# Linear attention: the denominators are read by VectorE ahead of phi's maximum instead of by ScalarE

## What is computed

```python
def elu_plus_one(x): return jax.nn.elu(x) + 1.0
sq = elu_plus_one(q)                            # q: 16 heads of 128
sk = elu_plus_one(k)                            # k, v: 4 heads, repeated over 16
kv = jnp.einsum('bhsd,bhse->bhde', sk, v)
qkv = jnp.einsum('bhsd,bhde->bhse', sq, kv)
k_sum = sk.sum(axis=2)
norm = jnp.einsum('bhsd,bhd->bhs', sq, k_sum)
attn = qkv / (norm[..., None] + EPS)            # EPS = 1e-6
return attn.transpose(0, 2, 1, 3).reshape(b, s, H * D) @ Wo.T
```

## Time and profile before

| | |
|---|---|
| median of 3 runs | 3480.19 us (3477.25 to 3481.44) |
| the profiled execution's own time | 3482.58 us |
| its span in the trace | 3480.7 us |
| mean granted TensorE clock | 0.986 |
| TensorE busy | 3326.6 us (96%), 19406 matmuls |
| VectorE busy | 2671.6 us (77%) |
| ScalarE busy | 2048.8 us (59%) |
| GpSimd busy | 1057.3 us (30%) |
| chain that ended last | TensorE 71%, VectorE 6%, ScalarE 3% of the span |

### The profile page before, as it was taken

One profiled execution on the slowest core, in us unless ns is written; L12 is line 12 of the kernel. 1 busy time (PEld: TensorE's weight loads), 2 busy tenths in 40 slices (PEclk: granted clock), 3 DMA queues, 4 the chain that ended last, 5 costly groups with the idle time before them and its releaser, 6 DMA issues.

```text
span 3480.7 us, 52744 instructions
## 1 busy us (share of the span) xinstructions
PE 3326.6 (96%) x19406; PEld 2853.0 (82%) x19406; DVE 2671.6 (77%) x4949; ACT 2048.8 (59%) x3904; POOL 1057.3 (30%) x1274
## 2 busy tenths in 40 slices
PE   4899999989999999999999999999999999999995
PEld 3778788768888888888888888888888888888884
DVE  5898896767876787876788677886788767876776
ACT  3677777645556565556555656555555565556552
POOL 4786667622222112122121222212212131212112
PEclk8999999999999999999999999999999999999997
DMA  2221122110000000000000001000000010001000
GB/s 85 73 81 58 54 66 73 50 37 13 13 22 29 15 13 13 15 25 25 13 13 13 28 26 33 13 16 25 25 13 16 14 32 25 16 19 31 27 17 20
DMA packets 98525, 104.21 MB, mean 30 GB/s; under 512 B 10336, under 2 KB 88800, under 8 KB 98144
## 3 DMA queue, kind: packets, MB, share of 16 engines
q1 hardware_dynamic: 98272, 100.85, 9.3%
HBM read 87.18 MB, written 13.63 MB: 29 GB/s over the span
## 4 chain that ended last, share of the span: by engine, by line
PE 71%; DVE 6%; ACT 3%; issue 0%; DMA 0%; POOL 0%; DVEq 0%; SPq 0%; ACTq 0%; POOLq 0%
PE at_ps_job L1965 12%; PE at_ps_job L35 7%; PE at_ps_job L37 7%; PE at_ps_job L36 7%; PE at_ps_o L35 6%; PE at_ps_o L37 6%; PE at_ps_o L36 6%; PE at_ps_s L35 6%; PE at_ps_s L36 6%; PE at_ps_s L37 6%; DVE at_neg_max L1892 1%; ACT x_resident L1716 1%; DVE at_probT_lo L1759 1%; PE at_ps_job L646 1%; DVE at_oT_lo L1790 0%; DVE ch_r L97 0%
## 5 line engine op out<-in xcount | busy, mean ns | idle before, releaser
L1675 ACT ACTIVATE at_probT_hi<-at_ps_job 128x512 fp32r<-128x512 f32 x1024 | 611.8, 598 | 888.9 <-PE at_ps_job L1965 886.5
L1759 DVE TENSOR_TENSOR at_probT_lo<-at_ps_job,at_probT_hi 128x512 fp32r<-128x512 f32 x1024 | 703.0, 687 | 274.8 <-ACT at_probT_hi L1675 264.6
L1716 ACT ACTIVATE x_resident<-at_ps_s,at_neg_max 128x1024 f32<-128x1024 f32 x512 | 570.9, 1115 | 151.4 <-DVE at_neg_max L1892 146.3
L1892 DVE TENSOR_REDUCE at_neg_max<-at_ps_s 128x1 f32<-128x1024 f32 x512 | 622.4, 1216 | 5.2
L1965 PE MATMUL at_ps_job<-ident,x_resident 128*128 128x128 f32 x4096 | 613.7, 272 | 5.0 <-DVE at_probT_lo L1759 3.2
L1965 PEld LDWEIGHTS at_ps_job<-ident,x_resident 128*128 128x128 f32 x4096 | 496.0, 140 | 97.7 <-issue 7.4
L35 PE MATMUL at_ps_o<-at_probT_hi,at_v_lo 128*128 128x512 f32 x1024 | 446.3, 436 | 8.9 <-DVE at_oT_lo L1790 7.8
L1651 POOL TENSOR_TENSOR at_w_hi<-at_w_raw,ch_cols 128x256 fp32r<-128x256 f32 x192 | 117.6, 613 | 1107.0 <-PE at_ps_job L37 1086.2
L35 PE MATMUL at_ps_s<-at_k_hi,at_q_lo 128*128 128x512 f32 x1024 | 445.1, 435 | 0.0
L37 PE MATMUL at_ps_o<-at_probT_lo,at_v_hi 128*128 128x512 f32 x1024 | 404.6, 395 | 0.0
L36 PE MATMUL at_ps_s<-at_k_hi,at_q_hi 128*128 128x512 f32 x1024 | 402.0, 393 | 0.0
(11 more groups left out here) (350 smaller groups left out, 7467.3 us busy)
## 6 DMA issues: line engine op xcount, KB each, us to landing
at_w_raw<-attn_w SPq DMA_DIRECT2D x256, 128.0 KB, 2.3
at_w_raw<-mlp_w SPq DMA_DIRECT2D x112, 128.0 KB, 2.3
li_wo_hi<-li_wo_kept SPq DMA_DIRECT2D x24, 256.0 KB, 2.6
li_wo_lo<-li_wo_kept SPq DMA_DIRECT2D x24, 256.0 KB, 3.0
li_wq_hi<-li_wq_kept SPq DMA_DIRECT2D x48, 128.0 KB, 2.1
li_wq_lo<-li_wq_kept SPq DMA_DIRECT2D x48, 128.0 KB, 2.3
x_resident<-x SPq DMA_DIRECT2D x4, 1024.0 KB, 12.6
out<-x_resident SPq DMA_DIRECT2D x4, 1024.0 KB, 5.0
```

The costliest lines, as they stand in the source:

```text
L1675: nc.scalar.activation(ph[:, i // TC, 4 * half:4 * half + 4, (i % TC) * P:(i % TC + 1) * P], c.turned_bank(2 * TB * u + 2 * i + half), ACT ...
L1716: nc.scalar.activation(prob[:, slot % 2, :], ps_s[slot % 2][:], ACT.Exp, bias=nmax[:, slot:slot + 1], accum_out=rsum[:, u % 2, slot:slot + ...
L1759: nc.vector.tensor_tensor(pl[at], c.turned_bank(2 * TB * u + 2 * i + half), ph[at].bitcast(F32), ALU.subtract).then_inc(s_pl, 1)
L1892: nc.vector.tensor_reduce(nmax[:, slot:slot + 1], ps_s[slot % 2][:], AX.X, ALU.max, negate=True).then_inc(s_max, 1)
```

## The change

The denominators are taken out of PSUM by VectorE (an addition of 1e-6 in place of ScalarE's copy with a bias), their reciprocal is made right behind that, and both now stand ahead of phi's maximum, so that VectorE waits for `s_y` (the end of the outputs' matmuls of the same step) before the maximum. ScalarE's instructions for the denominators go. `rnorm` gets two slots, by the parity of m, so the reciprocal waits for uses of two steps ago in place of those of one step ago. `s_norm` now counts tiles, four for each step.

```diff
-        rnorm = sb("rnorm", [P, TC], F32)
+        rnorm = sb("rnorm", [P, 2, TC], F32)
 # ScalarE
-                if y_step(t):
-                    act.wait_ge(s_y, t - LAG + 1)
-                    if t > LAG:
-                        act.wait_ge(s_rn, t - LAG)
-                    for own, banks in out_banks(t - LAG):
-                        last = nc.scalar.activation(norm[:, own], ps[:, banks, D], ACT.Copy, bias=ATT_EPS)
-                    last.then_inc(s_norm, 1)
...
-                    nc.scalar.activation(ybuf[:, m % 2, :], c.own_bank(("OUT", m, 3))[:, 0:D], ACT.Copy, scale=rnorm[:, 3:4]).then_inc(s_y3, 1)
+                    nc.scalar.activation(ybuf[:, m % 2, :], c.own_bank(("OUT", m, 3))[:, 0:D], ACT.Copy,
+                                         scale=rnorm[:, m % 2, 3:4]).then_inc(s_y3, 1)
 # VectorE
                 dve_background(nc, dve, sh, c, t)
+                if y_step(t):
+                    m = t - LAG
+                    dve.wait_ge(s_y, m + 1)
+                    for own, banks in out_banks(m):
+                        nc.vector.tensor_scalar(norm[:, own], ps[:, banks, D], ATT_EPS, None, ALU.add).then_inc(s_norm, own.stop - own.start)
+                    dve.wait_ge(s_norm, TC * (m + 1))
+                    if m >= 2:
+                        dve.wait_ge(s_y3, m - 1)
+                        dve.wait_ge(s_x, 3 * m - 3)
+                    nc.vector.reciprocal(rnorm[:, m % 2, :], norm[:]).then_inc(s_rn, 1)
                 if q_step(t):
                     dve.wait_ge(s_eq, t + 1)
                     nc.vector.scalar_tensor_tensor(f[:, t % 2, :], ...).then_inc(s_f, 1)
                 if y_step(t):
                     m = t - LAG
-                    dve.wait_ge(s_norm, m + 1)
-                    if m:
-                        dve.wait_ge(s_y3, m)
-                        dve.wait_ge(s_x, 3 * m)
-                    nc.vector.reciprocal(rnorm[:], norm[:]).then_inc(s_rn, 1)
                     dve.wait_ge(s_rn, m + 1)
                     for j in range(3):
                         x = x_tile_of(m, j)
-                        nc.vector.scalar_tensor_tensor(x, ..., rnorm[:, j:j + 1], x, ALU.mult, ALU.add).then_inc(s_x, 1)
+                        nc.vector.scalar_tensor_tensor(x, ..., rnorm[:, m % 2, j:j + 1], x, ALU.mult, ALU.add).then_inc(s_x, 1)
```

More of the change, by code:

```diff
@@ L1307, in _ @@
                         x = x_tile_of(m, j)
-                        nc.vector.scalar_tensor_tensor(x, c.own_bank(("OUT", m, j))[:, 0:D], rnorm[:, j:j + 1], x, ALU.mult, ALU.add).then_inc(s_x, 1)
+                        nc.vector.scalar_tensor_tensor(x, c.own_bank(("OUT", m, j))[:, 0:D], rnorm[:, m % 2, j:j + 1], x, ALU.mult, ALU.add).then_inc(s_x, 1)
         @block.tensor
```

## The result

The changed kernel takes 3470.47 us (median of 7 runs, 3467.94 to 3472.59) against 3480.35 us of the kernel before on the same chip: ratio 0.9971, 95% interval 0.9960 to 0.9981, so 9.9 us less. The forecast was 3481.2 us, the range began at 3471.0, and the time of the rival on the fast side was 3469. The phase behind the loop, and the clock (0.986 in both), are unchanged; the whole gain lies in the loop. Between the first and the last maximum it grows bit by bit: 0.8 us at step 8, 2.3 at step 43, 5.8 at step 71, 9.9 at the last.

A forecast was written before the change was run, and what follows sets the result against it. TensorE was taken to bound the loop at 93% busy, leaking at its wait for phi's maximum. Late steps +4.9, entries +1.1, closed output groups -2.4 and late exponentials -2.0 gave +1.6, taken as +1: 3481.2 us, range 3471 to 3491.

The forecast's parts named there:

- the rival on the fast side: Loop through ScalarE (maximum, copy, Relu, exponential) sets the pace, output groups close up: 12 us less, 3469 us, chance 0.13.
- the other 76: Of the loop's 128 steps, those where VectorE doesn't wait for the exponential and is late behind evictions and background work.
- 45 x 0.14 - 16 x 0.09 = +4.9 us: About 61 steps in late stretches that end in a TensorE wait: 45 without M longer, 16 with M shorter.
- The copy, the next step's Relu and exponential come 0.14 us earlier in a late step: ScalarE: phi's copy starts 0.78 us behind the maximum instead of 1.23, while the maximum starts 0.31 us later.
- nine steps, as -2.0 us: Gated steps with a late exponential: ScalarE's earlier copy gives up to 9 x -0.44 = -4.0 us; half taken.
- The terms of VectorE: Add to reciprocal 0.19 us, reciprocal to maximum 0.12, add to maximum 0.31 or 0.39, maximum to outputs 0.66.
- M: Eviction L1248, once in 32 steps: VectorE's wait for ScalarE's `m_hi` goes; -0.11 us per late step with it.
- The added wait: VectorE waits for the last output matmul (`s_y`) ahead of the maximum; the wait itself costs at most 0.07 us.
- TensorE's wait for `li_f` stays at 30 to 38 us: Sign to check: TensorE's wait for phi's maximum, 34.5 us before; a move over 7 us would refute the forecast.
- 44 us are all that any order of the other engines can give back: Loop with queries, 98 to 700 us: TensorE busy 557.75 of 602 us, so at most 44 us to gain.
- The slower one: VectorE's queue sets the late stretches and the added instructions are serial: 0.28 us per late step, 3491 us, chance 0.17.
- The lower bound: Added instructions free and all of the ScalarE gain arrives: -2.4 - 4.0 = -6.4 us, so 3474 us.

The follow-up runs named there:

- experiment 5: `ybuf` moved on ScalarE to just ahead of the next step's Relu: changed kernel 3472.92 us, kernel before 3465.04; behind the next exponential, kernel before: 3519.46.
- experiment 1's first kernel: Changed kernel with one wait more: ScalarE makes `ybuf`, and then phi's rounding copy, only behind the same step's maximum; 3489.04 us, ratio 1.0025.
- experiment 3: Halves of the change on the kernel before: reciprocal ahead of the maximum, ScalarE's copies kept, 3464.56 us; only the adds on VectorE, behind the maximum, 3494.58 us.

## Why the prediction was wrong, point by point

**"So in the other 76 it reaches the maximum late by itself."** This is the step that failed. I took VectorE's busy time for its work, and a late step's length for the sum of VectorE's own terms: "45 x 0.14 - 16 x 0.09 = +4.9 us". But VectorE's late arrival hangs in part on the maximum of the step before, through ScalarE. 76.6 us of its busy time was stretching, 36.9 of them until an end of GpSimd's that follows ScalarE's copy or `ybuf`, and another 14.0 us it waited for `m_hi`. Two views side by side would have shown it before the run: the durations of one form (L1291, 407 ns at the least, 590 in the median, 4802 at the most) and, for the long ones, GpSimd's timeline at the same microsecond.

**"The copy, the next step's Relu and exponential come 0.14 us earlier in a late step."** The number was right: the copy is 0.47 us nearer to a maximum that starts 0.28 to 0.35 later. The price was not: I gave it to nine steps, as -2.0 us, and nothing to the others. The forecast had a late step 0.14 us longer. Measured in the two traces, the steps that end in a maximum that TensorE waits for and in which VectorE is late by itself (31) are mostly 0.1 to 0.2 us shorter, 5.4 us in sum; those with a late exponential (10) are mostly 0.5 shorter, 3.4 us in sum, so of the "up to -4.0" nearly all arrived and not the half that I took; the other 86 give the last 1.1.

**The terms of VectorE.** Add to reciprocal 0.18 us (0.19 foretold), reciprocal to maximum 0.095 (0.12), first add to maximum 0.28 and with two adds 0.35 (0.31 and 0.39), maximum to outputs 0.637 (0.66). Each a little under, together 0.05 us in each late step, 3 us in all.

**M.** The wait ahead of L1248 was to fall from 14.0 us to under 5. It fell to 6.8, in 8 steps; the maximum to L1242 takes 1.90 us where it had been 2.38. Right in kind, and too small in price: I counted it in 16 steps, -0.09 us each, and experiment 5 gives 7.5 us for 0.36 us of `m_hi` in the changed kernel.

**The added wait.** 46.0 us for the last output matmul took the place of the wait for the exponential, and the sum is the same. As foretold, it costs nothing by itself. In the TensorE-paced step of the earlier trace rows the add starts at once behind the matmuls and the maximum 0.29 us later:

```profile
301.36 0.16 DVE L1292 TENSOR_SCALAR li_norm<-li_ps 128x4 f32<-128x4 f32 x1 [0.61 <-PE li_ps L37]
301.56 0.18 DVE L1297 RECIPROCAL li_rnorm<-li_norm 128x4 f32<-128x4 f32 x1
301.65 0.72 DVE L1300 SCALAR_TENSOR_TENSOR li_f<-li_ps,li_bias,li_f 128x512 f32<-128x512 f32 x1
```

**"TensorE's wait for `li_f` stays at 30 to 38 us."** It did, at 33.9, and it was no test: the gain passed by it, into TensorE's busy time. With that, "44 us are all that any order of the other engines can give back" falls too, since TensorE's 557.75 us held time in which its matmuls stood in a group.

**The rivals.** The faster one said that the loop through ScalarE sets the pace and the output groups close up, 46 x 0.27 = 12 us, 3469 in all, with a chance of 0.13. Its time and its groups were right (33 of them, by 0.21 us in most). Its loop was right as far as the copy; beyond it the way goes through GpSimd and through `m_hi`, where I had named Relu and the exponential. So its 3469 was in part luck: 46 x 0.27 = 12 us was built from the groups alone, and those of late steps closed by 0.2 in experiment 1's first kernel too, at 3489 us. What I held against it ("what TensorE gains it then waits for again") assumed that the next maximum doesn't move. The slower one, serial small instructions, was to decide from 0.45 us between add and maximum; 0.28 was measured. The rule that I had weighed for it (the Trainium skill, "VectorE: DVE Perf Modes", "Rules for kernel authors": keep the number of chained instructions low, since each empties the pipeline) doesn't bear out in the starts, 0.095 us apart for instructions of 0.18. Still, experiment 3 agrees with its advice: 171 small instructions more on VectorE cost 5.9 us, and 14.2 where they keep `ybuf` back.

**The range.** The lower bound was built from the small terms alone (-6.4 us, 3474), and the range was drawn 3 us below it, to 3471, to take in a part of the faster rival. The measured time lies 0.5 us below that. The bound was too near because a mechanism was missing, not because a duration was off.

## What to carry to other kernels

An engine's busy time can hold waiting: compare the durations of one form, and where they scatter, look at what the other engines do at that moment. Then follow what sets that moment back to your edit; here a copy and an eviction 0.47 us nearer to the maximum paid at VectorE, the copy in part through GpSimd, two engines on. But don't take the stretching for the gain: 67 us of it went with 3467, 3470 and 3489 us. And when a change does two things, price each alone: here the order was worth 16 us, and the work that was moved along with it cost 6.

## What the runs showed of the hardware

VectorE and GpSimd exclude each other in SBUF, sharply. In the kernel before, beside GpSimd's long instruction on x:

```profile
345.90 4.66 POOL L379 TENSOR_TENSOR x_resident<-x_resident,quant_bias_half 128x2048 f32<-128x2048 f32 x1
...
347.62 3.23 DVE L1291 SCALAR_TENSOR_TENSOR li_z<-li_z,li_ekk 128x256 f32<-128x256 f32 x1
```

VectorE's instruction takes 3.23 us instead of 0.41 and ends 0.28 us after GpSimd's (the records have 283 ns). It goes the other way too: GpSimd's `ybuf` addition, 0.72 us at the least and 0.75 in the median, takes 0.92 to 0.94 in the 38 cases in which it starts while an L1291 runs, 0.32 to 0.34 us before that ends. The 29 instances of L1291 that are stretched by over 0.2 us end 278 to 285 ns after one of GpSimd's; the 40 of the layer norm (L97) end 145 to 156 ns after one. L1291 reads two tensors from SBUF, L97 one. The lines that read PSUM with one SBUF tensor at most are never stretched in this trace, whatever GpSimd does: L1236 takes 652 to 693 ns 64 times, L1248 691 to 696 ns 32 times. The trace shows the stretching as busy time and as no wait at all.

The Trainium skill has the rule ("SBUF — State Buffer", "Who interferes with whom"): the two engines share one pair of SBUF ports, whoever comes first holds it for a whole instruction, and VectorE needs it when it reads two tensors from SBUF or runs in a two-port mode. The trace agrees with it in the lines above; that L97, with one tensor, is stretched would need a two-port mode, which no run here shows. What I had left undone was to ask the rule of the lines next to the edit.

Small VectorE instructions overlap: two adds follow each other by 0.04 to 0.08 us, mostly 0.07, where one alone takes 0.15, and the maximum starts 0.095 us after a reciprocal of 0.18.
